# A graph layer with a routed feed-forward: a unit's rank and list products a step later, in four list buffers

## The reference

```python
x = x + gnn(layernorm(x))        # write row y, 7 nearest nodes, GCNConv over the edges
x = x + ffn(layernorm(x))        # top-1 mixture of 8 experts, capacity ceil(1.25*T/8)

# in gnn
out = segment_sum(norm[:, None] * (mems2 @ W)[row], col) + (2*dinv*dinv)[:, None] * (mems2 @ W)
# in ffn
probs = softmax(x @ gate_w + gate_b); idx = argmax(probs)
pos = (cumsum(one_hot(idx), axis=0) * one_hot(idx)).sum(-1) - 1      # rank among the expert's tokens
buf[idx, pos] = x                                                    # only where pos < capacity
y = (relu(buf @ w1 + b1) @ w2 + b2)[idx, pos] * prob
```

## Time and profile before

| what | us |
|---|---|
| median of the runs shown (3 runs, 2759.76 to 2769.36) | 2766.18 |
| the profiled execution's own time | 2768.11 |
| its span, first to last instruction | 2766.6 |
| PE busy (matmuls) | 1982.8 (72%) |
| DVE busy | 1404.0 (51%) |
| POOL busy | 1609.1 (58%) |
| ACT busy | 583.3 (21%) |
| POOL's 1248 gathers of L676, busy | 1221.6 |

### The profile page before, as it was taken

How to read it: one execution, slowest core, us unless ns; L and a number is a source line. 1 busy time by engine, 2 the same in 40 slices (tenths; PEclk the granted TensorE clock), 3 DMA queues, 4 the chain that set the end, 5 groups by cost and what they waited for, 6 DMA issues and landing times. The chain is left out here.

```text
span 2766.6 us, 37885 instructions
## 1 busy us (share of the span) xinstructions
PE 1982.8 (72%) x11184; PEld 1704.9 (62%) x11185; DVE 1404.0 (51%) x3979; ACT 583.3 (21%) x1089; POOL 1609.1 (58%) x1646
## 2 busy tenths in 40 slices
PE   2002777776677667767777788878779899899985
PEld 1002555765466456656556677777668788788875
DVE  6999787236522641452342355555544344344442
ACT  0047100210021002002112132322223233233222
POOL 6741477777777777777777775655233422422233
PEclk8556898997899889889989988888889999999998
DMA  9116233663366346536646766655622212212121
GB/s 267 49 38 177 80 101 103 202 191 103 100 188 206 101 133 205 154 102 209 184 141 205 206 188 172 177 157 151 153 59 70 75 39 68 72 39 68 46 58 26
DMA packets 240377, 350.50 MB, mean 127 GB/s; under 512 B 47464, under 2 KB 173576, under 8 KB 240068
## 3 DMA queue, kind: packets, MB, share of 16 engines
q0 software_dynamic: 75712, 198.29, 24.8%
q1 hardware_dynamic: 163172, 148.02, 18.6%
q10 hardware_dynamic: 1312, 2.10, 0.2%
HBM read 296.73 MB, written 56.40 MB: 128 GB/s over the span
## 5 line engine op out<-in xcount | busy, mean ns | idle before, releaser
L676 POOL DMA_INDIRECT arena<-z_table,arena x1248 | 1221.6, 979 | 554.7 <-issue 365.8
L1765 PE MATMUL bank<-arena 128*128 128x128 f32 x4992 | 745.4, 312 | 338.3 <-DMA arena<-z_table,arena 180.8
L1765 PEld LDWEIGHTS bank<-arena 128*128 128x128 f32 x4992 | 690.7, 221 | 441.6 <-issue 371.1
L1232 DVE TENSOR_TENSOR nodes<-nodes,bank 128x256 f32 x312 | 131.5, 421 | 855.3 <-PE bank L1765 841.7
L736 POOL DMA_INDIRECT out<-arena x128 | 129.9, 1014 | 431.1 <-DVE arena L1645 413.7
L2011 PE MATMUL bank<-arena 128*128 128x256 f32 (+1 forms) x1472 | 329.8, 384 | 28.7 <-DVE arena L1592 17.8
L2023 PE MATMUL bank<-arena,nodes 128*128 128x256 f32 (+1 forms) x1472 | 326.0, 379 | 0.0
L2011 PEld LDWEIGHTS bank<-arena 128*128 128x128 f32 x1472 | 282.3, 196 | 69.8 <-issue 31.2
L795 ACT ACTIVATE arena<-arena 128x512 f32<-128x512 uint16 (+1 forms) x125 | 135.4, 1086 | 812.5 <-DVE arena L1251 460.2
L2023 PEld LDWEIGHTS bank<-arena,nodes 128*128 128x128 f32 (+1 forms) x1472 | 272.6, 187 | 40.1 <-issue 1.0
L898 ACT ACTIVATE nodes<-bank,arena 128x256 f32<-128x256 f32 (+1 forms) x368 | 152.7, 466 | 472.0 <-PE bank L2011 472.0
(11 more groups left out here) (308 smaller groups left out, 1926.4 us busy)
## 6 DMA issues: line engine op xcount, KB each, us to landing
arena<-z_table SPq DMA_DIRECT2D x120, 512.0 KB
arena<-z_table,arena POOLq DMA_INDIRECT x1248
arena<-in_L_ffn_w SPq DMA_DIRECT2D x14, 1024.0 KB, 7.5
z_table<-nodes SPq DMA_DIRECT2D x14, 896.0 KB, 6.7
x_rows<-nodes SPq DMA_DIRECT2D x98, 128.0 KB
arena<-in_x SPq DMA_DIRECT2D x48, 256.0 KB, 3.2
out<-nodes SPq DMA_DIRECT2D x96, 128.0 KB
nodes<-in_x SPq DMA_DIRECT2D x12, 896.0 KB, 11.5
```

The source lines that it names most:

```text
L676: nc.gpsimd.indirect_dma_start(gath[:, slot, t, :], None, z_table, bass.IndirectOffsetOnAxis(ap=src_idx[:, tile_at:tile_at + 1], axis=0)). ...
L1232: nc.vector.tensor_tensor(where, where, agg_bank[step % AB][:, 0:D].rearrange("p (k c) -> p k c", k=KD), ALU.add).then_inc(S["agg_added"], 1)
L1765: last = nc.tensor.matmul(agg_bank[i][:, k * P:(k + 1) * P], gath[:, i, t, k * P:(k + 1) * P], sel[:, i, t, :], start=(t == 0), stop=(t == ...
```

## The change

- The steps at which a unit's parts run are put into lists (`GATE_AT`, `CHOOSE_AT`, `RANK_AT`, `LIST_AT`) in place of offsets. For all units but unit 7: choose stays at f+1; rank and place go from f+2 to f+3; list blocks on DVE go from f+3 to f+4, two a step as before.
- PE's `list_rows` takes the blocks that DVE built in the step before, as before, but at the end of the step, behind group, conv and transposes, where it was the first thing in it. So the products of the blocks built at step s run at the end of step s+1.
- Unit 7 (batch 14, full at 310) goes to steps fixed by the last unit (LATE = 320): choose at 317, rank and place at 318, blocks at 318 and 319. Its exponential stays at 311.
- `list_lo` and `list_hi` have four buffers, and sit behind the gather and selection slots in the arena. DVE waits for a product only from a unit's fifth block on.
- In `node_work` place comes ahead of the list blocks. END is 327.
- SP stores the last units' marks first, then waits also for all list products, and only then loads expert 1's weights; `b2_rows` is still behind them.
- The clear of `gate_l` after the lists is waited for before its semaphore is raised.

```diff
@@ -135,6 +135,7 @@
     UW = 12
     UWIN = [(2 * FIRST[u[0]], 2 * FIRST[u[-1] + 1]) for u in UNIT_BATCHES]
     LW = 2
+    LB = 4
     BLOCK0 = [sum((b - a) // LW for a, b in UWIN[:u]) for u in range(NUN + 1)]
     NLB = BLOCK0[NUN]
 
@@ -142,14 +143,20 @@
         b = UNIT_BATCHES[u][-1]
         return begin(b) + 2 * PAIRS_IN[b] + 4
 
-    def units_at(step, after):
-        return [u for u in range(NUN) if full(u) + after == step]
-
-    def blocks_at(step, after):
+    LATE = full(NUN - 1)
+    GATE_AT = [full(u) for u in range(NUN)]
+    CHOOSE_AT = [full(u) + 1 if u != NUN - 2 else LATE - 3 for u in range(NUN)]
+    RANK_AT = [full(u) + 3 if u != NUN - 2 else LATE - 2 for u in range(NUN)]
+    LIST_AT = [full(u) + 4 if u != NUN - 2 else LATE - 2 for u in range(NUN)]
+
+    def units_at(step, when):
+        return [u for u in range(NUN) if when[u] == step]
+
+    def blocks_at(step):
         return [BLOCK0[u] + i for u in range(NUN) for i in range(BLOCK0[u + 1] - BLOCK0[u])
-                if full(u) + after + i // 2 == step]
-
-    END = full(NUN - 1) + 4 + (BLOCK0[NUN] - BLOCK0[NUN - 1] + 1) // 2
+                if LIST_AT[u] + i // 2 == step]
+
+    END = LIST_AT[NUN - 1] + 1 + (BLOCK0[NUN] - BLOCK0[NUN - 1] + 1) // 2
     NE = gate_w.shape[1]
     F = w1.shape[2]
     FT = F // P
@@ -352,8 +359,9 @@
         pick_cum = carve([NE, UW + 1])
         pick_u = carve([NE, UW + 1])
         go_on = carve([NE, UW + 1])
-        list_lo = carve([2, LW, P])
-        list_hi = carve([2, LW, NE, CT])
+        at[0] = GS * GT * D + SR * GT * P
+        list_lo = carve([LB, LW, P])
+        list_hi = carve([LB, LW, NE, CT])
         at[0] = x_ring_at
         rep_gath = carve([GT, D])
         rep_pick = carve([GT, P])
@@ -587,11 +595,12 @@
                             store_marks(u)
 
 
-            sp.wait_ge(S["agg_ps"], NG)
-            load_weights(1, 1)
             for u in range(NUN):
                 if UNIT_BATCHES[u][-1] + 3 >= NB:
                     store_marks(u)
+            sp.wait_ge(S["agg_ps"], NG)
+            sp.wait_ge(S["list_ps"], NLB)
+            load_weights(1, 1)
             sp.wait_ge(S["fixed"], 1)
             sp.dma_start(b2_rows, b2.rearrange("(o e) d -> o e d", o=1).to_broadcast([P, NE, D])).then_inc(S["w_small"], 16)
 
@@ -850,7 +859,7 @@
                     act.dma_start(w2_sb[:, 0, :, :], w2[0:1, :, :].rearrange("o (t p) d -> p (o t) d", p=P)).then_inc(S["w_in0"], 16)
                 for b, j in feats_of(step):
                     feat_pair(b, j)
-                for u in units_at(step, 1):
+                for u in units_at(step - 1, GATE_AT):
                     exp_unit(u)
                 for b in stats_of(step):
                     root_batch(b)
@@ -1386,11 +1395,12 @@
                 u = [u for u in range(NUN) if BLOCK0[u] <= n < BLOCK0[u + 1]][0]
                 a = (n - BLOCK0[u]) * LW
                 w = UWIN[u][0] + a
-                if n >= 2:
-                    dve.wait_ge(S["list_ps"], n - 1)
-                nc.vector.tensor_tensor(list_lo[:, n % 2, :, :], iota_r[:, :].unsqueeze(1).to_broadcast([P, LW, P]),
+                i = n - BLOCK0[u]
+                if n >= LB:
+                    dve.wait_ge(S["list_ps"], n - LB + 1 if i >= LB else BLOCK0[u])
+                nc.vector.tensor_tensor(list_lo[:, i % LB, :, :], iota_r[:, :].unsqueeze(1).to_broadcast([P, LW, P]),
                                         pos_lo[:, w:w + LW].unsqueeze(2).to_broadcast([P, LW, P]), ALU.is_equal).then_inc(S["list_in"], 1)
-                nc.vector.tensor_tensor(list_hi[:, n % 2, :, :, :], unit_row[:, a:a + LW, :].unsqueeze(3).to_broadcast([P, LW, NE, CT]),
+                nc.vector.tensor_tensor(list_hi[:, i % LB, :, :, :], unit_row[:, a:a + LW, :].unsqueeze(3).to_broadcast([P, LW, NE, CT]),
                                         unit_tile[:, a:a + LW, :].unsqueeze(2).to_broadcast([P, LW, NE, CT]), ALU.mult).then_inc(S["list_in"], 1)
 
             def routing_ready():
@@ -1411,15 +1421,15 @@
                     stats_batch(b)
                 for b in norms_of(step):
                     newton_batch(b)
-                for n in blocks_at(step, 3):
+                for u in units_at(step, RANK_AT):
+                    place_unit(u, step)
+                for n in blocks_at(step):
                     list_block(n)
-                for u in units_at(step, 2):
-                    place_unit(u, step)
-                for u in units_at(step, 1):
+                for u in units_at(step, CHOOSE_AT):
                     choose_unit(u)
                 for b, j in logits_of(step):
                     take_logits(b, j, step)
-                for u in units_at(step, 0):
+                for u in units_at(step, GATE_AT):
                     gate_unit(u)
 
             dve.wait_ge(S["counts_clear"], 1)
@@ -1580,7 +1590,8 @@
             then(nc.vector.scalar_tensor_tensor(list_f[:, :], list_bank[:, 0:P], -1.0, list_f[:, :], ALU.add, ALU.add))
             then(nc.vector.tensor_copy(list_i[:, :], list_f[:, :]))
             dve.sem_inc(S["list_ok"], 1)
-            nc.vector.memset(gate_l, 0.0).then_inc(S["gate_in"], 1)
+            then(nc.vector.memset(gate_l, 0.0))
+            dve.sem_inc(S["gate_in"], 1)
 
 
             def feats(q, s, took):
@@ -1889,17 +1900,17 @@
                 last.then_inc(S["rank_ps"], 1)
 
             def list_rows(n, r):
+                u = [u for u in range(NUN) if BLOCK0[u] <= n < BLOCK0[u + 1]][0]
+                j = (n - BLOCK0[u]) % LB
                 pe.wait_ge(S["list_in"], r * (2 * R_BLOCKS) + 2 * (n + 1))
                 for i in range(LW):
-                    last = nc.tensor.matmul(list_bank[:, 0:NE * CT], list_lo[:, n % 2, i, :],
-                                            list_hi[:, n % 2, i, :, :].rearrange("p e t -> p (e t)"),
+                    last = nc.tensor.matmul(list_bank[:, 0:NE * CT], list_lo[:, j, i, :],
+                                            list_hi[:, j, i, :, :].rearrange("p e t -> p (e t)"),
                                             start=(n == 0 and i == 0), stop=(n == NLB - 1 and i == LW - 1))
                 last.then_inc(S["list_ps"], 1)
 
             def node_step(step, r):
 
-                for n in blocks_at(step, 4):
-                    list_rows(n, r)
                 if step < NG:
                     i = step % BODY
                     pe.wait_ge(S["sel_ok"], r * R_STEPS + (step + 1))
@@ -1909,11 +1920,11 @@
                     pe.wait_ge(S["agg_added"], min(step - AB, NG - 1) + NP + 1)
                 for b, j in logits_of(step - AB):
                     pe.wait_ge(S["gate_taken"], r * R_PAIRS + (FIRST[b] + j + 1))
-                for u in units_at(step - AB, 2):
+                for u in units_at(step - AB, RANK_AT):
                     pe.wait_ge(S["rank_taken"], r + (u + 1))
                 for b, j in logits_of(step):
                     logit_pair(b, j, step, r)
-                for u in units_at(step, 2):
+                for u in units_at(step, RANK_AT):
                     rank_unit(u, step, r)
                 if step < NG:
                     add_up(step % BODY)
@@ -1921,6 +1932,8 @@
                     convolve(b, j, r)
                 for b, j in turns_of(step):
                     turn_pair(b, j, r)
+                for n in blocks_at(step - 1):
+                    list_rows(n, r)
 
             pe.wait_ge(S["w_conv"], 4 * 16)
             nc.tensor.transpose(turn_bank[:, 0:NE * FT], b1_rows[0:NE * FT, :], ident[0:NE * FT, 0:NE * FT]).then_inc(S["b1_ps"], 1)
```

## The result

| what | before | after |
|---|---|---|
| median of the runs shown, us | 2766.21 (4 runs, 2759.76 to 2769.36) | 2700.61 (4 runs, 2694.01 to 2703.07) |
| profiled execution / its span, us | 2768.11 / 2766.6 | 2703.07 / 2701.5 |

The ratio is 0.9762, with a 95% interval of 0.9737 to 0.9787: 65.6 us less. The forecast was 2693 us. Medians are over all executions shown; the ratios leave out two slow ones (4007.35 us, the kernel before in the last group of experiments, and 2925.53 us, e12).

What follows compares the result with a forecast made beforehand. The loop PE, DVE, PE was taken to bound steps 260 to 311. Terms of -76.8, +2 and +1 us gave -73.8 from the profiled 2768.1 us, or 2694.3; allowing for the lower median, 2693 us, range 2683 to 2717.

Steps and rivals of the forecast that it cites:

- 55 steps: From group 256 to group 311: 363.9 us, 6.6 a step, would fall to 287.1 us, 76.8 us less.
- routing in the tail: Step 311 to the experts' first transposes: unit 7's moved work costs 2 us more; bounds 4 less and 6 more.
- first token rows: First token gathers after the lists, now beside SP's weight loads: 1 us more, bounds 0 and 15 us.
- The bound and its successor: Steps 260 to 311: the loop PE, DVE, PE bounds; then POOL at 41.8 us a unit, PE 3.2 us under.
- The waits in units 0 to 6: PE's rank and list waits and the slow rows behind them go: 13.4 us a unit, from 54.3 to 40.9.
- a distance longer by those 4.0 us: List products behind group, conv and mostly a transpose gain 4.0 us of distance, against a longest wait of 5.8 us.
- 5.22 us a step: POOL's pace as next bound in the 55 steps: four gathers of 1.004 us with 0.30 us of issue each.
- signs of being wrong: Unit over 44 us, POOL waiting for PE, list products waiting at step ends, first token row over 5 us to ACT.
- The rival with both loads in full, 15 us: After the lists: token gathers stand behind SP's loads, 15 us in place of 1, or `b2_rows` late; 2707 us, chance 0.08.
- Rival 1: Units' steps: rank wait goes, half the list waits and slow rows stay; 5.8 us a step, 2723 us, chance 0.17.
- Rival 3: Group steps: pauses in every step drop PE's clock for good; 70 us a unit, 2886 us, chance 0.02.
- Rival 4: Each step: a wait for ACT's copy or the gathers grows by what was removed; about 2766 us, chance 0.02.

Runs made afterwards that it cites:

- e12: Changed kernel with list blocks one a step in units 0 to 6, SP's weights behind bias rows and first tokens, last unit's rank and lists a step earlier: 2690.26 us.
- e2: Changed kernel with the list products back at the head of PE's step, ahead of the group; later steps and four buffers kept: 2764.43 us.
- e6: Changed kernel with POOL issuing three gathers a step, not four, from step 268 on; output not the layer's: 2669.05 us.
- e1: Changed kernel with rank products and lists back at their earlier steps; list products still behind the group, four buffers kept: 2696.12 us.
- e3: Changed kernel with two list buffers in place of four: 2696.01 us.
- e4: Changed kernel with unit 7 chosen, ranked and listed at its own steps, as units 0 to 6 are: 2691.77 us.
- e10: Kernel before with only the list products moved from the head to the end of PE's step: 2698.38 us.
- e11: Changed kernel with list products at the head of PE's step, but two steps behind their blocks: 2702.87 us.
- e5: Changed kernel with SP's load of expert 1's weights put behind the bias rows and the first four half rows of tokens: 2694.84 us.
- e7: Changed kernel with list blocks of units 0 to 6 one a step over six steps, not two a step over three: 2685.23 us.

## Why the prediction was right, and where it wasn't

The terms of the sum against the profiled executions:

| term | predicted | measured |
|---|---|---|
| 55 steps | -76.8 | -68.9 |
| routing in the tail | +2 | +0.4 |
| first token rows | +1 | +2.8 |
| not in the sum: start of group 256 | 0 | +0.9 |
| not in the sum: from ACT's first token rows on | 0 | -0.4 |
| sum | -73.8 | -65.2 |

**The bound and its successor.** Right, and shown. The loop PE, DVE, PE held the steps (e2 restores it: waits of 45.5 us, and 355 us); with it open POOL's gathers are the bound (e6), and PE is close under it. The prediction put PE at 38.6 us a unit, 4.8 a step; e6 runs at 4.58. It had taken the list product (1.38 us) and the rank product (0.98) from rows behind waits; without a wait they are 0.89 and 0.51 from start to start, 2 us less a unit.

**"The waits in units 0 to 6".** The waits went, as counted, but I gave the gain to all of them and to the later step. e1 keeps the rank product's waits (16.8 us in 7) and loses nothing; e3 and e4 take two more parts away and lose nothing; e10 has the place alone and has all of the gain. Of the 13.4 us a unit that I removed, 2.6 (the rank wait) lay in slack once the lists no longer closed the loop. It made no difference to the number, because the pace came from POOL and not from that subtraction. My reason for the list products ("a distance longer by those 4.0 us") is what e11 confirms: distance is what counts.

**The step that was mis-sized: "5.22 us a step".** It was 5.36 (294.9 / 55). I had taken 1.004 us for a gather beside routing from a stretch of before where POOL was mostly waiting; in the changed kernel it is 1.033 us. Over 220 gathers that is 6.4 of the 7.9 us missed. The excess over 0.955 us was 8.4 us before and 17.8 after: more of POOL's gathers met DVE's runs. Part of that is chance: with the same list instructions the mean gather is 1.012 us in e4, 1.015 in e5, 1.016 in e3 and 1.036 in e11, all above the 0.992 of the kernel before over these steps. That POOL meets DVE's runs more often because it no longer waits fits these means and is not shown by an experiment. The last group came at 1905.8 us where about 1897 was forecast.

**The tail.** The routing in batch 16's pause was taken as +2 and came as +0.4 (lists 43.7 to 44.1 us after group 311). But the same tail code gives 42.5 to 44.9 us over the runs, so terms of 2 us are not settled by one profile. e1 had them at 41.8 with the last unit a step earlier, e12 at 42.5, as e7 without it.

**The weights.** "I take 1 us" was too small: 2.8 us in the profiled pair, 3 to 4 over the runs (e5). I priced it by the gathers under SP's stores at step 256; the right neighbour was not in the trace, and PE's pause in that row is charged to issue, not to a gather. One of my signs of being wrong did show here: the first pair of gathers reached ACT 5.27 us after POOL had issued it, over the 5 that I had named, against 2.49 before and 3.17 in e5. The error is small in the sum all the same. The rival with both loads in full, 15 us, didn't come. The Trainium skill (DMA: Bandwidth & Descriptors, "Queues, rings and completion order") has a DMA engine take turns between queues; that agrees with a cost between nothing and 15 us, and gives no size.

**The rivals.** Rival 1 (5.8 us a step, 2723 us) didn't come: PE's list waits are 0.7 us, not half of 45.5. Rival 3, the clock falling for good, neither: the granted clock rose from 0.85 to 0.92 over 1640 to 1900 us, although PE waited for gathers 7 times, up to 3.2 us. What pauses of 2 us do was left open. Here the length of the pause alone doesn't tell: behind waits of 3.22 and 2.27 us the next groups took 3.51 and 3.76 us, behind one of 1.89 us the group took 2.03, and behind one of 1.00 us 2.89. The first of them:

```profile
1723.87 1.84 PE L1888 MATMUL bank<-arena 128*128 128x8 f32 x8 [3.22 <-DMA arena<-z_table,arena]
...
1726.52 3.51 PE L1776 MATMUL bank<-arena 128*128 128x128 f32 x16
```

The Trainium skill (TensorE: Matmul & The Clock Gate, "HAM oscillation") warns of pauses in every tile; here they are in few of the steps, and the slow groups with them; no run has a pause in every step. Rival 4, a gain that another wait takes up, didn't come either: PE's new waits for gathers are 10.4 us, where POOL's for PE fell by 75.9.

## What to carry to other kernels

When two engines feed each other in every step, look at where in the consumer's program order the product stands: at the head, for what was built in the step before, it puts the consumer's main work into the loop. Moving it behind that work, or one step further, opened the loop here at no cost that the profile shows (e10, e11); four buffers and a later step for everything together didn't (e2). Before you count on the next bound's pace, ask what that engine will collide with once it no longer waits.

## What the runs showed of the hardware

An indirect gather that POOL issues is held back by a run of DVE instructions with both inputs in SBUF. Alone it takes 0.95 us; started together with two, four or eight such instructions of 0.33 us each it takes 1.57, 2.23 and 3.57 us, ending about 0.8 us after the last of them. Reductions of the same length, with one input, don't hold it (0.82 us after the two-input work, in their midst). The nine gathers over 2 us in 55 steps of the changed kernel are 11.2 us longer than nine of 0.955 us would be. A single such instruction does it too: `select`, 0.68 us, held the gather shown above to 1.20 us, ending 0.83 us after it. The Trainium skill (SBUF — State Buffer, "Who interferes with whom") says that a DVE instruction with two SBUF inputs contends with a GpSimd instruction that reads SBUF, and calls the contention an exclusive lock. The lengths agree, with one thing more: a gather is held over a whole row of such instructions, not over one. The same section says that `tensor_tensor` was not seen to stall DMAs from that engine; here it does stall gathers with indices in SBUF, and the measurement decides. That the reading of the indices is the point where they meet is a guess that no run tested.
